# One scale for all experts, their largest weights taken in the convolution's fourth batch, and two chunks turned ahead

## The reference

```python
xn = ln_c(x)                                   # over the 256 channels
attn = softmax(relu(bn(conv1x1(relu(conv7x7_dilated2(xn))))))   # 49 taps per pixel
x = x + sum(patch(xn, p) * attn[:, p] for p in range(49))
t = tokens(x)                                  # 4 batches of 2304 tokens, 256 channels
n = layernorm(t)
weights = softmax(capacity_scaled(softmax(mean(n, tokens) @ Wr + br)))   # per batch
top_w, top_i = top_k(weights, 2); top_w = softmax(top_w)
y = sum(top_w[k] * (gelu(n @ W1[e] + b1[e]) @ W2[e] + b2[e]) for k, e in enumerate(top_i))
out = t + layernorm(y + n) * gamma + beta
```

## Time and profile before

| | us |
|---|---|
| median of 3 runs | 1045.54 |
| lowest, highest | 1044.06, 1052.4 |
| the profiled execution | 1043.68 |
| its span, first to last instruction | 1041.9 |
| PE busy | 956.7 (92%) |
| DVE busy | 731.0 (70%) |
| ACT busy | 541.2 (52%) |
| POOL busy | 144.5 (14%) |

### The profile page before, as it was taken

One profiled execution on the slowest core, in us unless ns is written; L12 is line 12 of the kernel. 1 busy time (PEld: TensorE's weight loads), 2 busy tenths in 40 slices (PEclk: granted clock), 3 DMA queues, 4 the chain that ended last, 5 costly groups with the idle time before them and its releaser, 6 DMA issues. The chain is left out here.

```text
span 1041.9 us, 19437 instructions
## 1 busy us (share of the span) xinstructions
PE 956.7 (92%) x7649; PEld 736.9 (71%) x7649; DVE 731.0 (70%) x1826; ACT 541.2 (52%) x963; POOL 144.5 (14%) x163
## 2 busy tenths in 40 slices
PE   2777999999999999999998837999999999999997
PEld 1676666776677667668998714777777787777776
DVE  4776466488558636466657656689869987998767
ACT  5685333435345322235454237576766767586751
POOL 1100100000000020201111210111211121122111
PEclk9999999999999999999998858999999999999999
DMA  9531111012202110114554360331242124212101
GB/s 243 173 92 46 47 46 47 24 51 86 65 2 78 33 42 26 46 34 107 151 168 138 93 178 1 84 90 42 58 126 62 32 61 123 62 34 60 46 17 46
DMA packets 89692, 77.08 MB, mean 74 GB/s; under 512 B 24604, under 2 KB 86445, under 8 KB 89502
## 3 DMA queue, kind: packets, MB, share of 16 engines
q1 hardware_dynamic: 79680, 66.32, 23.2%
q10 hardware_dynamic: 9920, 9.51, 3.0%
HBM read 46.42 MB, written 29.40 MB: 73 GB/s over the span
## 5 line engine op out<-in xcount | busy, mean ns | idle before, releaser
L1237 PE MATMUL pM<-V,U 128*128 128x368 f16 (+3 forms) x2016 | 319.4, 314 | 0.0
L1237 PEld LDWEIGHTS pM<-V,U 128*128 128x128 f16 x2016 | 194.3, 97 | 100.5
L1727 ACT ACTIVATE gf<-pH,b1c,sc 128x384 f32<-128x384 f32 x192 | 128.0, 669 | 109.9 <-issue 89.6
L1921 DVE SCALAR_TENSOR_TENSOR gl<-gf,sc,gh 128x384 f16<-128x384 f32 x192 | 146.2, 792 | 43.7 <-ACT gh L1718 43.2
L2078 PE MATMUL pY<-w2h,gl 128*128 128x256 f16 x576 | 157.0, 273 | 0.0
L2078 PE MATMUL pY<-w2l,gh 128*128 128x256 f16 x576 | 157.0, 273 | 0.0
L2078 PE MATMUL pY<-w2h,gh 128*128 128x256 f16 x576 | 157.0, 273 | 0.0
L2062 PE MATMUL pH<-xh,w1h 128*128 128x384 f16 x384 | 127.1, 331 | 6.4 <-DVE w1l L1880 5.6
L2062 PE MATMUL pH<-xl,w1h 128*128 128x384 f16 x384 | 126.9, 330 | 0.0
L2062 PE MATMUL pH<-xh,w1l 128*128 128x384 f16 x384 | 126.8, 330 | 0.0
L700 ACT CAST V<-pV 128x384 f16<-128x384 f32 x96 | 45.6, 478 | 155.1 <-PE pV L1208 155.0
(11 more groups left out here) (260 smaller groups left out, 1468.9 us busy)
## 6 DMA issues: line engine op xcount, KB each, us to landing
xa<-in_xt SPq DMA_DIRECT2D x16, 576.0 KB, 6.2
xs_scratch<-xs SPq DMA_DIRECT2D x16, 576.0 KB, 4.4
tk<-t_scratch SPq DMA_DIRECT2D x24, 384.0 KB, 3.5
out<-o SPq DMA_DIRECT2D x24, 384.0 KB, 2.7
U<-xs_scratch SPq DMA_DIRECT2D x16, 480.0 KB, 4.4
w1r<-in_ew SPq DMA_DIRECT2D x8, 512.0 KB, 4.2
w2r<-in_ew SPq DMA_DIRECT2D x8, 512.0 KB, 6.3
V<-in_w1g SPq DMA_DIRECT2D x5, 784.0 KB, 15.8
```

What stands on the lines that cost most here:

```text
L1237: return nc.tensor.matmul(out[:, :, first:end], U[:, k, hi_u, piece, :], V[:, b % 2, hi_v, k, c, :, first + TILES * d:end + TILES * d], st ...
L1727: nc.scalar.activation(gf[:, (JB * m + j) % GBUFS, :], pH[:, (JB * m + j) % HBUFS, 0:CN], ACT.Gelu, bias=b1c[:, j // FB, j % FB:j % FB + 1 ...
L1921: stt(gl[:, sl, j, :], gf[:, (JB * m + j) % GBUFS, :], scale_of(b, G_UP), gh[:, sl, j, :], ALU.mult, ALU.subtract).then_inc(g_step, 1)
```

## The change

- `spread_table` and `G` get 128 rows (rows 113 to 127 are zero); the products still use 113.
- In the fourth batch SP loads all weights of all eight experts, as 19 units, through three buffers in `xs1`: units 0 to 7 are W1 of each expert, 8 is all b1, 9 to 16 W2, 17 and 18 the b2 (broadcast to 128 partitions). The load of unit u waits until unit u - 3 is taken. They stand behind the load of `G` and ahead of all `load_back`.
- DVE takes each unit's largest magnitudes (`take_unit`) at the end of the slots 2 to 8: 2, 3, 3, 3, 4, 2, 2 units.
- PE sums them over the partitions in one matmul, in the list of image 14; DVE copies the sums at the end of the stage.
- PE transposes the last batch's statistics ahead of the last sums and not behind them.
- The second stage has one set of scales for all batches: `scales()`, 11 steps, first in DVE's list. `largest_w1`, `largest_w2`, `bound`, `scales_1`, `scales_2` and their waits in `turn_x` and `layer1` are gone.
- ACT: the exponentials, chunk 0 normalised between the second and the third, then chunk 0 evicted, chunk 1 normalised and evicted, then W1 split. The high half of W2 for batch 0 is made by DVE (`split_w2(0, high=True)`), for the others by ACT as before.
- PE: chunks 0 and 1 are both transposed ahead of layer1(0, 0). The router's products use banks of `pY`.
- `b1c` is copied between the two low halves of W1, and ACT's first Gelu waits for it alone and no more for the sum of b2.
- SP: beta and gamma go out ahead of the experts' loads and not behind them; b2 goes last, with a semaphore of its own.

```diff
@@ spread_table, G @@
-    g = np.zeros((LO + TAPS, len(EDGE) + 1, GW), np.float16)
+    g = np.zeros((P, len(EDGE) + 1, GW), np.float16)
...
@@ mix_phase @@
+        stage = [xs_all[:, k * 4 * C * 2:(k + 1) * 4 * C * 2].bitcast(F32) for k in range(STAGES)]
...
@@ mix_phase, sync @@
             sp.dma_start(G[:, :, :], spread_d).then_inc(g_loaded, 16)
             for s in range(2):
                 sp.wait_ge(xs_stored[s], 16 * IMGS // 2)
+            sp.wait_ge(v_turned, V_TURNS * IMGS)
+            for u in range(UNITS):
+                if u >= STAGES:
+                    sp.wait_ge(unit_taken, u - STAGES + 1)
+                src, dst = unit(u)
+                sp.dma_start(dst, src).then_inc(unit_loaded[u % STAGES], 16)
             for n in range(XB):
                 load_back(n)
...
@@ mix_phase, vector @@
+            def take_unit(u):
+                dve.wait_ge(unit_loaded[u % STAGES], 16 * (u // STAGES + 1))
+                nc.vector.tensor_reduce(largest[:, u:u + 1], unit(u)[1] if u == EXPERTS else stage[u % STAGES],
+                                        AX.XY if u == EXPERTS else AX.X, ALU.max, apply_absolute_value=True).then_inc(unit_taken, 1)
...
                         if k < NP - 1:
                             spread_low(early_items(k, 1))
+                        first = sum(UNITS_SLOT[s] for s in UNITS_SLOT if s < k)
+                        for u in range(first, first + UNITS_SLOT.get(k, 0)) if b == B - 1 else ():
+                            take_unit(u)
...
+            dve.wait_ge(units_summed, 1)
+            nc.vector.tensor_copy(wsum[:, :], pC[:, SUMS_AT:SUMS_AT + UNITS]).then_inc(wsum_taken, 1)
...
@@ mix_phase, tensor @@
+                if n == IMGS - 2:
+                    pe.wait_ge(unit_taken, UNITS)
+                    nc.tensor.matmul(pC[:, SUMS_AT:SUMS_AT + UNITS], ones[:, :], largest[:, :],
+                                     start=True, stop=True).then_inc(units_summed, 1)
...
             sum_added(B - 1)
+            turn_stats(B - 1)
             sum_tokens(IMGS - 1)
             sum_shifts(B - 1)
-            turn_stats(B - 1)
...
@@ ffn_phase, sync @@
             for m in range(2):
                 load_chunk(0, m)
+            sp.dma_start(bet[:, :], beta.broadcast_to([P, C])).then_inc(gb_loaded, 16)
+            sp.dma_start(gam[:, :], gamma.broadcast_to([P, C])).then_inc(gb_loaded, 16)
             sp.wait_ge(r_step, 16)
             load_experts(0)
-            sp.dma_start(bet[:, :], beta.broadcast_to([P, C])).then_inc(gb_loaded, 16)
-            sp.dma_start(gam[:, :], gamma.broadcast_to([P, C])).then_inc(gb_loaded, 16)
...
@@ ffn_phase, scalar @@
+            for k in range(2):
+                act.wait_ge(r_step, (2, 11)[k])
+                nc.scalar.activation(r[:, 2 * k + 1, :], r[:, 2 * k, :], ACT.Exp).then_inc(r_exp, 1)
             normalise(0, 0)
+            act.wait_ge(r_step, 17)
+            nc.scalar.activation(rc[:, 5:6], rc[:, 4:5], ACT.Exp).then_inc(r_exp, 1)
+            nc.scalar.activation(rc[:, 7:8], rc[:, 4:5], ACT.Gelu)
+            take_x(0, 0)
             normalise(0, 1)
-            take_x(0, 0)
+            take_x(0, 1)
             split_w1(0)
-            act.wait_ge(bias_step, 3)
+            act.wait_ge(bias_step, 1)
             gelus(0, 0)
-            take_x(0, 1)
-            act.wait_ge(r_step, R_STEPS + 1)
-            split_w2(0)
             normalise(0, 2)
...
@@ ffn_phase, vector @@
+            scales()
             dve.wait_ge(r_pe, 1)
...
-            take_x(0, 0)
-            largest_w1(0)
-            scales_1(0)
+            take_x(0, 1)
             split_w1(0)
             split_hidden(0, 0, range(JB))
-            take_x(0, 1)
-            largest_w2(0)
-            scales_2(0)
-            split_w2(0)
+            split_w2(0, high=True)
             split_b2(0)
...
@@ ffn_phase, tensor @@
             turn_x(0, 0)
-            pe.wait_ge(xl_ready, 1)
-            bound(0, 0)
+            pe.wait_ge(r_step, R_STEPS)
+            nc.tensor.matmul(pY[:, 2, 0:TOPK * B], ones[0:B, :],
+                             wdiag[:, :, :].rearrange("p b k -> p (b k)"),
+                             start=True, stop=True).then_inc(r_pe, 1)
+            turn_x(0, 1)
             layer1(0, 0)
-            turn_x(0, 1)
-            bound(0, 1)
+            pe.wait_ge(r_step, R_STEPS + 1)
```

More of the change, by code:

```diff
@@ L76 @@
 SIG_STEPS = 7
+EXPERTS = 8
+B2_UNITS = 2
+UNITS_1, UNITS = EXPERTS + 1, 2 * EXPERTS + 1 + B2_UNITS
+STAGES, UNITS_SLOT = 3, {2: 2, 3: 3, 4: 3, 5: 3, 6: 4, 7: 2, 8: 2}
+SUMS_AT = 448
 class Steps:
@@ L407, in mix_phase @@
         mean_step = sem("mean_step")
+        unit_loaded = [sem(f"unit_loaded{s}") for s in range(STAGES)]
+        unit_taken = sem("unit_taken")
+        units_summed = sem("units_summed")
+        wsum_taken = sem("wsum_taken")
         stats_turned = sem("stats_turned")
@@ L524, in third, with unit @@
             return range(k * NT // 3, (k + 1) * NT // 3)
+        def unit(u):
+            ew1, eb1, ew2, eb2 = experts
+            here = stage[u % STAGES]
+            if u in (EXPERTS, UNITS_1 + EXPERTS, UNITS_1 + EXPERTS + 1):
+                if u == EXPERTS:
+                    return eb1.rearrange("e p f -> p e f"), here[:, 0:EXPERTS * 4].rearrange("p (e f) -> p e f", e=EXPERTS)
+                part, h = EXPERTS // B2_UNITS, u - UNITS_1 - EXPERTS
+                return eb2.rearrange("(h e) c -> h (e c)", e=part)[h:h + 1].broadcast_to([P, part * C]), here[:, 0:part * C]
+            e, w = (u, ew1) if u < EXPERTS else (u - UNITS_1, ew2)
+            return w[e].rearrange("(f p) c -> p f c", p=P), here.rearrange("p (f c) -> p f c", f=w.shape[1] // P)
         def load_w(eng, g):
@@ L1483, with ffn_phase @@
 Z_ALL = 5 * CT + 1
-def ffn_phase(nc, mean, consts, t_d, stat_d, ew1, eb1, ew2, eb2, gamma, beta, out):
+def ffn_phase(nc, mean, wsum, consts, t_d, stat_d, ew1, eb1, ew2, eb2, gamma, beta, out):
     ident, wrs, brs = consts
@@ L1572, in ffn_phase, with scale_of @@
         out_stored = [sem(f"out_stored{s}") for s in range(2)]
[L1574 to L1580, removed]
+        def scale_of(what, n=1):
+            return sc[:, what:what + n]
         block = ctx.enter_context(nc.Block())
@@ L1618, in load_experts @@
                                  ).then_inc(w2_loaded, 16)
+                for k, e in enumerate(chosen):
+                    sp.dma_start(b2r[:, k], eb2[ds(e, 1), :].broadcast_to([P, C])).then_inc(b2_loaded, 16)
             def ew_b(eb1, e):
@@ L1677, in _ @@
         def _(act):
[L1678 to L1684, removed]
             def split_w1(b):
@@ L1882, in split_w1 @@
-                dve.wait_ge(b_loaded, 64 * (b + 1))
-                if not is_first(b):
-                    dve.wait_ge(gelu_done, JB * CHUNKS * b)
-                s.did(nc.vector.tensor_copy(b1c[:, :, :], b1r[:, :, :]))
+                    stt(w1l[:, k], w1r[:, k], scale_of(W1_UP), w1h[:, k], ALU.mult, ALU.subtract).then_inc(w1_step, 1)
+                    if k == 0:
+                        dve.wait_ge(b1_loaded, 32 * (b + 1))
+                        after(dve, gelu_done, JB * CHUNKS * b)
+                        s.did(nc.vector.tensor_copy(b1c[:, :, :], b1r[:, :, :]))
@@ L2032, in turn_x @@
                 after(pe, xl_ready, n)
-                if m == CHUNKS - 1 and later(b, m, 1, CHUNKS):
-                    pe.wait_ge(sc_step, SC_STEPS * (b + 1) + SC1_STEPS)
-                if m == 0 and not is_first(b):
-                    pe.wait_ge(sc_step, SC_STEPS * (b + 1))
                 for c in range(CC):
@@ L2041, in turn_x @@
                     last.then_inc(x_turned, 1)
-            def bound(b, part):
-                pe.wait_ge(max_step, MAXES * b + (TOPK + 1) * (part + 1))
-                to = bounds(b, part)
-                nc.tensor.matmul(to, ones[:, :], mxs[:, part, :],
-                                 start=True, stop=True).then_inc(bound_ready, 1)
             def layer1(b, m):
@@ L2051, in layer1 @@
                 pe.wait_ge(xl_ready, n + 1)
-                if m >= CHUNKS - 2 and later(b, m, 2, CHUNKS):
-                    bound(b + 1, m - CHUNKS + 2)
                 for j in range(JB):
@@ L2114, in program @@
         mix_phase(nc, xt, w1g, b1, w2, b2, bn_gamma, bn_beta, bn_mean, bn_var, ident_d, spread_d, data_d, tap_d, xs_d, attn_d, ln_d, t_d, stat_d,
-                  mean, ident, const_loads)
-        ffn_phase(nc, mean, consts, t_d, stat_d, ew1, eb1, ew2, eb2, gamma, beta, out)
+                  mean, ident, const_loads, (ew1, eb1, ew2, eb2), largest, wsum)
+        ffn_phase(nc, mean, wsum, consts, t_d, stat_d, ew1, eb1, ew2, eb2, gamma, beta, out)
 def kernel(**inputs):
```

181 lines of the change are left out of this document (71 added, 110 removed).

## The result

The changed kernel takes 1035.13 us (median of 4 runs, 1032.06 to 1035.75), the kernel before beside it 1044.8 us; the ratio is 0.9882 with a 95% interval of 0.985 to 0.9915. Forecast were 1037 and a range of 1028 to 1044. Six further runs of it on another chip gave 1036.48 us, eleven of the kernel before there 1046.63 us, ratio 0.9907 (0.988 to 0.9934). Its profiled execution took 1035.75 us, span 1034.0.

The account below looks back on a forecast made before the run. PE was taken to bound the convolution, with DVE's work free while PE's next spread finds its bank empty. Head with barrier -14.7, changes of batch -2.6, new matmul +0.2, fourth batch +9.4 make -7.7 us: 1037 us, range 1028 to 1044.

Parts of the forecast that it names:

- the three places: Where time counts: slots 2 to 8 of the fourth batch, the second stage's head, the three changes of batch.
- The barrier: End of the first stage: statistics transposed first, so the store leaves earlier; 1.3 us gained, bounds nothing and 1.9 us.
- The head: Second stage's start: first product at 614.8, not 620.35; layer2 at 634.4, not 649.15; 14.7 us gained including 1.3 us of barrier.
- The changes of batch: Second stage, between batches: six bound matmuls and their waits leave PE; 2.6 us gained, bounds 1.2 and 3.3.
- The fourth batch: First stage: DVE's reductions do not fit its idle time and PE stalls; 9.4 us lost, bounds 6.0 and 15.5.
- The stall: Fourth batch: PE waits at its fourth spread for DVE's late low half; 6.3 us, bounds 4.0 and 10.1 us.
- the low clock: Behind the fourth batch's stall: 4 to 6 us at half rate, 2.0 to 3.0 us lost, 2.5 taken.
- Rival A: Fourth batch: reductions stay hidden because DVE catches up or loads land sooner; about 1028 us, chance 0.12.
- Rival B: Fourth batch: the table's load stays on one DMA engine and units queue behind it; 1057 us, chance 0.05.
- Rival C: Fourth batch: unit loads take 7 us or more each, using up the head's gain; about 1044 us, chance 0.13.
- The signs: Expected in the profile: table load within 6 us, DVE idle below 1 us in 401 to 425, PE idle 5 to 8 us.
- The total: Whole kernel: all terms together -7.7 us, forecast 1037 us.

Follow-up runs that it names:

- experiment 8: Changed kernel with only the last statistics transposition put back behind the sums; 1.84 us from the means to the next stage, 0.51 us in the changed kernel.
- experiment 9: Changed kernel with the beta and gamma loads back behind the experts' loads; first product at 16.1 us, layer2 at 35.3 us; further parts edit W2 and token sums.
- the part of experiment 9 on W2: Changed kernel with W2's high half for the first batch back on ACT; 1042.97 us, layer2 of the first chunk at 41.3 us.
- Experiments 1 to 3: Changed kernel with units spaced over slots 2 to 10 (1031.77 us), reductions reading 32 of 1024 columns (1030.8 us), or only three units loaded (1030.76 us).
- experiment 4: Changed kernel with the spread table back at 113 rows; 1051.97 us.
- experiment 5: The changed kernel again, unedited, as the measure for the next experiment on the same chip; 1036.48 us, ratio 0.9907 to the kernel before.
- experiment 1: Changed kernel with the 19 units spaced over slots 2 to 10, one in slot 6 and not four; 1031.77 us, ratio 0.9844 to the kernel before.

## Why the prediction was right, point by point

The direction, the three places and the mechanism in each were right; several sizes inside the sum were off, and that the head came out so near has some luck in it.

**The barrier**: 1.3 us forecast, 1.34 us in the traces, and experiment 8 gives just that back. Not in the forecast: the transposition no longer stands behind the sums, so the whole move is worth 1.6 us.

**The head**: forecast 16.5 us to the first product and 36.1 us to layer2, measured 16.2 and 36.2. Single terms were off and partly cancelled. ACT normalised chunk 0 at 5.8 us from the stage's start (forecast 5.7). The low half of W1 was put at 1.7 us because of POOL; it took 1.28, and experiment 9 shows that the earlier load of beta, which was given as the reason for less than 2.8 us, has no part in it: behind the experts' loads the additions would have come too late to meet it. W2's high half on DVE was bounded by half of 1.27 us from below; it took 0.75 us. That this work went from ACT to DVE was told as a detail; the part of experiment 9 on W2 shows it to be worth 5 to 6 us.

**The changes of batch**: 2.6 us forecast, 3.0 in E.

**The fourth batch** was right in mechanism and too high in size: 9.4 us against 7.3, inside its bounds of 6.0 and 15.5. (The stall's own bounds have small slips: 6.3 less 2.1 is 4.2 and not 4.0, and 6.3 with 2.1 and 2 more is 10.4 and not 10.1.) Two terms make the difference. The stall was 4.9 us over the old wait and not 6.3: DVE's sums ended 0.5 us sooner than forecast (on the batch's own clock), the steps from there to the first low half took 0.4 us less, and PE was itself 0.4 us late by then. And the low clock cost 1.65 us, not 2.5: the stretch of the earlier trace rows behind 3.68 us of idle lasted 6 us, this one 3.7 us from PE's return. Experiments 1 to 3 show that the mechanism is this one: without DVE's time the batch costs 98.68 us as before, loads or no loads; with four units in slot 6 about half of the stall is the load that can start only when a buffer comes free there.

**Rival A**, reductions hidden, was the wrong forecast for this kernel but is nearly true with another distribution of the units (0.7 us in B). **Rival B**'s mechanism is real, as experiment 4 shows, for 113 rows; its price was put at 30 us in the batch (27 up to the first spread, 3 behind it), and B measured 24.8 us. **Rival C** did not come: the units took 4.6 us and not 7.

**The signs.** Of those that were named, PE's stall (5.53 us), the low clock behind it, DVE's wait for a load in slot 6 (1.73 us), both times of the head and the absence of waits behind it came. Two did not. The table's load took 10.5 us and not under 6, with the units loading beside it. And DVE was idle for 2.9 us and not under 1 between 401 and 425, so the units did not fill every gap even there.

**The total**: -7.7 us forecast, -9.7 us between the medians. The trace moved by 7.9 us, but with 3.6 us more in A, in code that was not touched; that this is so near the forecast is chance. In the parts that the change touches, B, D, E and the barrier, the traces give 7.3 - 13.2 - 3.0 - 1.3 = -10.2 us.

## What to carry to other kernels

Work that is put into the idle time of an engine off the critical path fits by the gap it falls into and not by its sum: count the idle time up to the next point where the critical engine waits for that engine, and if several loads share few buffers, leave at most as many units in one slot as there are buffers. A PE stall can cost its length and then the low clock behind it: here every stall read from 2.94 to 6.11 us was followed by low clock, and none of those of 0.40 to 0.81 us in the fourth batch was. So a small overrun on another engine can cost more than double (2.2 us of ACT cost 5 to 6 us in layer2's place). And look at a transfer's row count before queueing others behind it: a 113-row load was harmless as long as nothing urgent followed.

## What the runs showed that I had not expected

The clock of PE also falls without any idle time. In the kernel before, 20 products of one column each (token sums) end near 504.9, and the products behind them run at half rate:

```profile
502.57 2.36 PE L1361 MATMUL pA<-U,V 120*128 120x1 f32 x20
504.79 0.52 PE L1342 MATMUL pM<-U,V 120*120 120x256 f16 x3
505.14 0.80 PE L1342 MATMUL pM<-U 120*120 120x256 f16 x3
505.74 1.27 PE L1342 MATMUL pM<-U,V 120*120 120x256 f16 x5
...
509.10 0.71 PE L1342 MATMUL pM<-U,V 120*120 120x256 f16 x5
```

PE counts as busy throughout; five such products take 1.27 us, and 0.71 us again from 509 on. Where and how often this happens changes from run to run: one fall in 490 to 560 us in the profile of the changed kernel, two in that of experiment 5, five in that of experiment 1, whose C is 7.6 us longer than the changed kernel's. In the thirteen traces with all sums, every fall in this stretch comes within 5 us of the start of twenty such products; but most such groups in the changed kernel's trace are followed by none. It goes with the time of single runs: in experiment 1 the run of 1027.32 us had a mean clock of 0.977, the one of 1034.88 us 0.969. That low clock is what makes such runs differ is likely, and not shown. A stretch that no edit touches, A, moved by 6.4 us between traces; one trace against another proves no small gain there.
